# Moving the second norm's row scaling and the shift of the eight largest scores from VectorE to GpSimd, with the orders of four engines rewritten

## The reference, cut to what matters

```
h = layernorm(x) * (1 + ca) + sa
x = x + ga * attention(rmsnorm(h) * norm_w)     # 16 heads of 64, causal, gated by sigmoid(x @ Wg)
h = layernorm(x) * (1 + cb) + sb                # (x - m) / sqrt(v + 1e-5): the second norm
x = x + gb * (mlp(h) + experts(h))
```

## Time and profile before

| | us |
|---|---|
| median of 3 runs (lowest, highest) | 1511.75 (1511.45, 1513.72) |
| the profiled execution's own time | 1514.42 |
| its span from first to last instruction | 1512.6 |
| busy: PE, PE weight loads | 1405.7, 1151.4 |
| busy: DVE, ACT, POOL | 1356.1, 1242.2, 1082.9 |
| mean granted TensorE clock, share of full | 0.976 |

### The profile page before, as it was taken

One profiled execution on the slowest core, in us unless ns is written; L12 is line 12 of the kernel. 1 busy time (PEld: TensorE's weight loads), 2 busy tenths in 40 slices (PEclk: granted clock), 3 DMA queues, 4 the chain that ended last, 5 costly groups with the idle time before them and its releaser, 6 DMA issues.

```text
span 1512.6 us, 39371 instructions
## 1 busy us (share of the span) xinstructions
PE 1405.7 (93%) x11361; PEld 1151.4 (76%) x11361; DVE 1356.1 (90%) x5366; ACT 1242.2 (82%) x4103; POOL 1082.9 (72%) x1201
## 2 busy tenths in 40 slices
PE   3789999999999999999999999999999999999963
PEld 2567888887788887778888777887887788788742
DVE  5579999999999999999999999999999999999853
ACT  1788888988888898888889888888988888888831
POOL 2017877777787777778777777877777787777786
PEclk7999999999999999999999999999999999999976
DMA  5000000000000000000000000000000000000000
GB/s 129 15 13 6 20 20 19 16 19 14 9 19 19 19 16 19 14 9 19 19 19 16 19 14 9 19 19 19 16 19 14 9 19 19 19 16 12 13 8 7
DMA packets 50880, 27.86 MB, mean 18 GB/s; under 512 B 10304, under 2 KB 50048, under 8 KB 50848
## 3 DMA queue, kind: packets, MB, share of 16 engines
q1 hardware_dynamic: 50608, 27.05, 6.9%
q10 hardware_dynamic: 240, 0.43, 0.1%
HBM read 23.15 MB, written 4.31 MB: 18 GB/s over the span
## 4 chain that ended last, share of the span: by engine, by line
PE 60%; DVE 25%; issue 5%; ACT 5%; POOL 3%; DMA 1%; DVEq 0%; POOLq 0%; ACTq 0%
PE pS L1054 9%; PE pW L996 9%; PE pW L998 7%; PE pW L997 7%; PE pW L1067 6%; PE pS L1044 5%; DVE pS L764 5%; DVE h L862 5%; PE pS L1040 4%; ACT pS L534 4%; PE pW L1128 4%; PE pW L1131 4%; PE pW L1071 2%; DVE p_sb L784 2%; PE pW L1119 2%
## 5 line engine op out<-in xcount | busy, mean ns | idle before, releaser
L534 ACT ACTIVATE pS<-pS,nmx 128x128 f32<-128x128 f32 (+1 forms) x1024 | 390.4, 441 | 53.7 <-DVE nmx L764 53.7
L427 POOL TENSOR_TENSOR fexp<-fexp,fsum 128x512 f32<-128x512 f32 x256 | 320.6, 1283 | 80.6 <-DVE fexp L900 80.6
L764 DVE CUSTOM_DVE_ANT_0 pS<-pS,mask 128x128 f32<-128x128 f32 (+1 forms) x1024 | 330.1, 390 | 23.3 <-PE pS L1044 22.8
L418 POOL TENSOR_TENSOR fsum<-ex 128x512 f32<-128x512 f32 x256 | 257.6, 1043 | 0.0
L526 ACT COPY pT<-pS 128x768 f32<-128x768 f32 x256 | 211.7, 827 | 36.0 <-PE pS L1054 31.5
L1054 PE MATMUL pS<-ident,p_sb 128*128 128x128 f32 x1536 | 216.3, 277 | 10.4 <-DVE p_sb L784 6.5
L784 DVE TENSOR_TENSOR p_sb<-pS,coef 128x256 f32<-128x256 f32 (+2 forms) x512 | 210.5, 453 | 8.9
L1054 PEld LDWEIGHTS pS<-ident,p_sb 128*128 128x128 f32 x1536 | 173.3, 141 | 41.5 <-issue 13.5
L534 ACT ACTIVATION_READ_ACCUMULATOR pS<-pS,nmx 128x1 f32 x1024 | 202.2, 197 | 0.0
L434 POOL TENSOR_TENSOR fexp<-fexp 128x512 f32<-128x512 f32 x128 | 172.1, 1364 | 0.2
L516 ACT COPY qk<-pW 128x512 f32<-128x512 f32 x256 | 166.7, 651 | 6.0 <-PE pW L998 6.0
(11 more groups left out here) (164 smaller groups left out, 3642.0 us busy)
## 6 DMA issues: line engine op xcount, KB each, us to landing
x_in<-in_L_attn_tokens SPq DMA_DIRECT2D x32, 128.0 KB, 2.1
modA<-mods_dram SPq DMA_DIRECT2D x32, 128.0 KB, 3.1
x_res<-in_L_attn_tokens SPq DMA_DIRECT2D x32, 128.0 KB, 3.0
modB<-mods_dram SPq DMA_DIRECT2D x32, 128.0 KB, 2.9
out<-yo SPq DMA_DIRECT2D x32, 128.0 KB, 1.9
modC<-mods_dram SPq DMA_DIRECT2D x32, 64.0 KB, 3.0
fsum<-in_L_attn_Wkv SPq DMA_DIRECT2D x2, 512.0 KB, 6.5
fsum<-in_L_attn_Wq SPq DMA_DIRECT2D x1, 512.0 KB, 4.7
```

Source lines behind the costliest of these rows:

```text
L418: ins = nc.gpsimd.tensor_tensor(fsum[:, k, h], ex[:, k, h, 0:NX].unsqueeze(2).broadcast_to([P, NX, NK]), ex[:, k, RH + h, :].unsqueeze(1). ...
L427: ins = nc.gpsimd.tensor_tensor(fexp[:, k, h, :], fexp[:, k, h, :], fsum[:, k, h].rearrange("p i j -> p (i j)"), ALU.mult)
L534: ins = nc.scalar.activation(ps, ps, ACT.Exp, bias=nmx[:, p % 2, h, k:k + 1], scale=-1.0, accum_out=den(p)[:, h, k:k + 1])
L764: ins = nc.vector.tensor_tensor_reduce(out=ps, in0=ps, in1=mask[:, (1 - k) * P:2 * P], scale=-1.0, scalar=LARGEST, op0=ALU.add, op1=ALU.mi ...
```

## The change

`ln2_modulate` disappears from DVE. POOL's `rstd2` becomes `normalise2`, which also does the two row-block instructions. DVE's `shift` no longer makes `top_d`; POOL's new `shift_tops` does, started by a semaphore that the MAX8 instructions set. The orders of DVE, ACT and PE and the bank table are rewritten; POOL's order only gains `shift_tops` after `rms1`. The helper semaphores change to match (`rstd2_out` goes, `pool_chain2` counts 2, `top_s_ready` is new, `HEAD_LINKS` 4 becomes 2).

```diff
@@ GpSimd
+                def shift_tops():
+                    if w.live(-1):
+                        pool.wait_ge(S(top_s_ready), at(top_s_ready, f, TB))
+                        t = top_s[:, :, :, :].rearrange("p a h n -> p (a h) n")
+                        nc.gpsimd.tensor_tensor(top_d[:, :, :, :].rearrange("p a h n -> p (a h) n"), t, t[:, :, 0:1].broadcast_to([P, 2 * TB * RH, TK]),
+                                                ALU.subtract).then_inc(S(top_d_ready), 1)
...
-                        nc.gpsimd.tensor_tensor(rs2[:, :], ve2[:, :], expo[:, :], ALU.pow).then_inc(S(rstd2_out), 1)
+                        nc.gpsimd.tensor_tensor(rs2[:, :], ve2[:, :], expo[:, :], ALU.pow).then_inc(S(pool_chain2), 1)
+                        pool.wait_ge(S(pool_chain2), at(pool_chain2, f, 2))
+                        apart()
+                        for k in range(TB):
+                            ins = nc.gpsimd.tensor_scalar(h2[:, k, :], x2[:, k, :], mv2[:, k, 0:1], rs2[:, k:k + 1], ALU.subtract, ALU.mult)
+                        ins.then_inc(S(h2_ready), 1)
...
-                rstd2()
+                normalise2()
                 weigh(1)
                 rstd1()
                 add_heads(1)
                 rms1()
+                shift_tops()
                 fold(1)
@@ VectorE
-                def ln2_modulate():
-                    if w.live(-1):
-                        dve.wait_ge(S(rstd2_out), at(rstd2_out, f, 1))
-                        for k in range(TB):
-                            ins = nc.vector.tensor_scalar(h2[:, k, :], x2[:, k, :], mv2[:, k, 0:1], rs2[:, k:k + 1], ALU.subtract, ALU.mult)
-                        ins.then_inc(S(h2_ready), 1)
...
-                        link(ins, head_chain, f)
+                        ins.then_inc(S(top_s_ready), 1)
+                        dve.wait_ge(S(top_s_ready), at(top_s_ready, f, k + 1))
...
-                        if k == TB - 1:
-                            nc.vector.tensor_tensor(top_d[:, :, :, :], top_s[:, :, :, :], top_s[:, :, :, 0:1].broadcast_to([P, 2, TB * RH, TK]),
-                                                    ALU.subtract).then_inc(S(top_d_ready), 1)
-                            done(head_chain)
```

More of the change, by code:

```diff
@@ L190, in program @@
         rstd1_in, rstd1_out = ev("rstd1_in", 2), ev("rstd1_out", 2)
-        pool_chain1, pool_chain2 = ev("pool_chain1", 2), ev("pool_chain2", 1)
+        pool_chain1, pool_chain2 = ev("pool_chain1", 2), ev("pool_chain2", 2)
         xr_ready = ev("xr_ready", 1)
@@ L198, in program @@
         x2g_ready = ev("x2g_ready", 1)
-        rstd2_in, rstd2_out = ev("rstd2_in", 1), ev("rstd2_out", 1)
+        rstd2_in = ev("rstd2_in", 1)
         h2_ready = ev("h2_ready", 1)
-        top_d_ready, tops_ready = ev("top_d_ready", 1), ev("tops_ready", 1)
+        top_s_ready, top_d_ready, tops_ready = ev("top_s_ready", TB), ev("top_d_ready", 1), ev("tops_ready", 1)
         cand_ready, rz_ready = ev("cand_ready", 1), ev("rz_ready", 1)
@@ L211, in program @@
         y_gated = ev("y_gated", 1)
-        order = [("V", 0, 0), ("QK", 2, 0), ("QK", 3, 0), ("V", 3, 0), ("PV", 6, -1), ("GU", 1, -2),
[5 rows of a table removed]
+        order = [("V", 0, 0), ("PV", 6, -1), ("QK", 2, 0), ("V", 3, 0), ("QK", 3, 0), ("GU", 1, -2),
[5 rows of a table added]
         assert len(order) % NW == 0, len(order)
@@ L463, in rms1, with normalise2 @@
                         nc.gpsimd.tensor_tensor(rr1[:, :], me1[:, :], expo[:, :], ALU.pow).then_inc(S(rstd1_out), 1)
-                def rstd2():
+                def normalise2():
                     if w.live(-1):
@@ L619, in body @@
                 copy_transposes(7, -1)
+                values(0)
+                weighted(6)
                 queries(2)
-                values(0)
+                values(3)
+                exp_scores(0)
                 queries(3)
-                exp_scores(0)
-                weighted(6)
-                values(3)
                 gate_up(1)
@@ L628, in body @@
                 weighted(7)
+                values(1)
+                scale_head(1)
                 down_tanh(0)
-                scale_head(1)
                 copy_transposes(0, 0)
+                copy_transposes(1, 0)
                 down_tanh(1)
-                copy_transposes(1, 0)
+                values(4)
                 gate_up(2)
-                values(1)
                 exp_scores(2)
@@ L639, in body @@
                 exp_scores(3)
-                copy_transposes(2, 0)
                 weighted(1)
+                gate_up(3)
                 queries(4)
                 scale_head(3)
-                gate_up(3)
+                copy_transposes(2, 0)
                 queries(5)
+                values(2)
                 copy_transposes(3, 0)
-                values(4)
                 modulate_h()
@@ L650, in body @@
                 exp_scores(4)
+                exp_scores(5)
+                weighted(2)
+                weighted(3)
+                scale_head(5)
                 queries(6)
-                weighted(2)
-                values(2)
-                exp_scores(5)
+                values(5)
                 queries(7)
-                values(5)
-                scale_head(5)
-                weighted(3)
                 copy_transposes(4, 0)
@@ L661, in body @@
                 total(1)
+                experts(0)
                 weighted(4)
@@ L664, in body @@
                 rms_scale()
-                experts(0)
                 expert_exp(1)
@@ L668, in body @@
                 weighted(5)
+                exp_scores(6)
                 experts(1)
-                exp_scores(6)
                 exp_scores(7)
@@ L856, in ln2_stats @@
                         ins.then_inc(S(rstd2_in), 1)
-                def ln2_modulate():
-                    if w.live(-1):
-                        dve.wait_ge(S(rstd2_out), at(rstd2_out, f, 1))
-                        for k in range(TB):
-                            ins = nc.vector.tensor_scalar(h2[:, k, :], x2[:, k, :], mv2[:, k, 0:1], rs2[:, k:k + 1], ALU.subtract, ALU.mult)
-                        ins.then_inc(S(h2_ready), 1)
+                        done(head_chain)
                 def shift(k):
@@ L926, in body @@
                 normalise(1)
+                choose(1, 0)
                 gated_down(0)
-                choose(1, 0)
+                choose(1, 1)
+                row_max(2)
+                bias_product(2)
+                row_max(3)
                 gated_down(1)
-                row_max(2)
-                row_max(3)
-                bias_product(2)
+                gate_product(2)
+                ln2_stats()
                 normalise(2)
-                ln2_stats()
-                gate_product(2)
-                choose(1, 1)
                 normalise(3)
                 ln1_stats()
-                ln2_modulate()
                 bias_product(3)
@@ L945, in body @@
                 normalise(4)
+                normalise(5)
                 shift(0)
-                normalise(5)
                 ln1_modulate()
@@ L954, in body @@
                 finish()
+                normalise(7)
                 bias_product(0)
-                normalise(7)
                 gate_product(0)
@@ L1138, in body @@
                 transpose_scores(7, -1)
+                weigh_values(6)
                 project_qk(2)
-                project_qk(3)
                 project_v(3)
                 scores(1)
-                weigh_values(6)
+                project_qk(3)
                 gate_up(1)
+                project_v(1)
                 weigh_values(7)
                 project_down(0)
-                project_v(1)
                 transpose_scores(0, 0)
+                project_v(4)
                 project_down(1)
@@ L1156, in body @@
                 weigh_values(1)
-                transpose_scores(2, 0)
                 project_qk(4)
@@ L1160, in body @@
                 project_qk(5)
-                project_v(4)
+                project_v(2)
+                transpose_scores(2, 0)
+                transpose_h()
                 transpose_scores(3, 0)
                 scores(4)
-                transpose_h()
                 scores(5)
                 weigh_values(2)
+                weigh_values(3)
                 project_qk(6)
-                project_v(2)
                 similarity(0)
@@ L1171, in body @@
                 project_qk(7)
-                weigh_values(3)
                 transpose_scores(4, 0)
-                similarity(1)
                 transpose_scores(5, 0)
                 transpose_experts(0)
+                similarity(1)
                 weigh_values(4)
@@ L1181, in body @@
                 transpose_x()
+                project_ffn(0)
                 transpose_experts(1)
-                project_ffn(0)
                 project_ffn(1)
@@ L1194, in _ @@
             run(pe, body)
-LN1_LINKS, ATTN_LINKS, HEAD_LINKS, TAIL_LINKS, SU_LINKS = 4, NP, 4, 2, 8
```

(1 more changed line is left out.)

## The result

The changed kernel took 1518.07 us (median of 5 runs, 1517.76 to 1519.3) against 1511.93 for the kernel before in the same session: ratio 1.0036, 95% interval 1.0025 to 1.0048. It is slower by 0.4%, beyond the 0.2% that can be told. I had forecast 1503 and a gain. The time lies inside the wide range that I gave (1486 to 1521), but on its slower side.

A forecast was written before the change was run, and what follows sets the result against it. No engine was free: PE allowed about 1.0 us a step, lost on a DVE stretch held up by POOL. A step of 44.15 less 0.25 to 0.3, over 32 steps, gave 8.6 us: 1511.75 to 1503, range 1486 to 1521.

The forecast's parts named there:

- signs of being wrong: h2's instructions near 0.74 us or more, L828 to L833 long, masks still 0.54, or PE idle before similarity(0) or scores.
- The walk: One step followed from scores 1 to scores 6: ln2_stats 1.4 us later, h2 1.7 earlier, scores 6 at 723.3 against 723.61.
- I take 0.40, near the low end: POOL's price in us for each of two 128x128 h2 instructions; 0.80 for both, range 0.68 to 1.48.
- a lead of 0.3: PE reaches scores 6 0.3 us sooner; carried over, a step is 0.25 to 0.3 us shorter.
- The estimate by the Trainium skill: GpSimd at about twice VectorE's time: 1.36 us for the h2 pair, losing up to 0.4 us a step.
- Removed from DVE, 3.6 us: h2's two instructions (2.32 us) and top_d (1.27) leave DVE's 41.9 us a step, leaving about 38.3.
- The masks: choose(1,1) before rm2 meets POOL's large instructions: four masks take 4.4 us instead of 3.1, ln2_stats 1.4 us later.
- Rival (a): Masks held up less than walked, only ACT and PE bound: 0.6 to 0.9 us a step gained, 1483 to 1493; chance 0.22.
- Rival (c): Masks held up in full, POOL's later additions may meet ln1_modulate: slower, likely 1518 to 1528, at most 1540; chance 0.21.
- top_d: On POOL 0.45 us, delaying fold(1) by 0.5; covered by ET1 behind the first half of the feed-forward matmuls (1.8 us).
- ACT's copy before V5: PE waits 0.35 us for V5's bank before scores 6, since PV2's copy now stands behind exponentials 5.
- Filling and draining: Outside the steady steps: same pieces at uncovered prices, DVE's 0.32 against POOL's 0.40; under 1 us, taken as nothing.

The follow-up runs named there:

- after_h_half: Changed kernel with each h2 instruction on GpSimd doing 64 of the 128 columns, the other half of h2 a constant; 1503.96 us, ratio 0.9942.
- after_mask_late: Changed kernel with choose(1,1), the second pair of masks, moved from in front of row_max(2) to behind normalise(3); 1505.74 us, ratio 0.9956.
- after_pv2_early: Changed kernel with ACT's copy of PV2 in front of the exponentials of pair 5 instead of behind them; 1518.00 us, ratio 1.0031.
- after_h_on_dve: Changed kernel with h2 done by DVE again, behind ln1_stats, and rstd2 on POOL; 1611.53 us, ratio 1.0641.
- both_old_order: Kernel before with both moves (h2 and top_d to GpSimd), its old orders and bank table kept; 1516.52 us, ratio 1.0030.

## Why the prediction was wrong

The sign was wrong: faster was forecast, by 0.25 to 0.3 us a step, and it is 0.3 slower. Of the signs of being wrong that I had named, the first came: h2's instructions at 0.74 or more. The walk can be checked point by point. Scores 1 start at 692.32 in the kernel before and 691.80 after, so the changed kernel's times are moved by 0.52 us:

| event | before | forecast | measured, moved |
|---|---|---|---|
| row maximum 2 starts | 701.46 | 703.2 | 703.07 |
| ln2_stats starts | 705.81 | 707.2 | 706.84 |
| PE starts on h | 712.77 | 711.0 | 711.64 |
| exponentials 4 start | 714.89 | 714.6 | 715.15 |
| scores 6 start | 723.61 | 723.3 | 723.91 |

**The step that failed** is one term of the sum, "I take 0.40, near the low end, since only one operand is a tensor; 0.80 for both". It is 0.804 each, 1.60 for both. Up to ln2_stats the walk is right within 0.4 us and on the late side; at h it is 0.6 too early, and this error stands nearly unchanged at exponentials 4 and scores 6 and turns a lead of 0.3 into a lag of 0.3. From ln2_stats to h I had walked 3.8 us and it is 4.8: 0.8 of that is the pair, the rest small excesses in the statistics, the roots and the waits between them. after_h_half changes the pair alone: 0.43 us less in it brings the step 0.46 down, below the kernel before. Each instruction is beyond my upper row too (739 for two tensor operands of twice the size): the reason given, one tensor operand, was no reason. The estimate by the Trainium skill, GPSIMD Engine Reference, section "Performance versus the Vector engine", 1.36 for the pair, was nearer than mine, and the runs exceed it too. I had written that by it the lead would lose up to 0.4 a step; that sentence alone would have led to no gain. My range for the term did end at 1.48, where by the same walk the lead is gone too (0.68 us more than I took, against a lead of 0.28).

**Removed from DVE, 3.6 us: right.** L862 and L878 are gone, and the rest of their cost was the wait for POOL's instructions: undone in the new orders, either is long again.

**The masks: right in size, too weakly drawn.** 4.4 us for four was walked, 4.43 measured, and ln2_stats came 1.0 later against 1.4 forecast. But the experiment says that this one move costs 12 us, nearly as much as after_h_half takes away. Rival (a) put a kernel with less waiting there 0.6 to 0.9 us a step below the kernel before, which is 0.3 to 0.6 below my walk; after_mask_late is 0.38 below the changed kernel. Rival (c), longer waits for the masks, did not occur; its other part, ln1_modulate meeting POOL's later additions, left a trace (the pair took 0.73 instead of 0.60) and no more; its two-input additions (now L843, L844) ran while POOL was waiting and kept their 0.42. So the result lies where rival (c) had its likelier half (1518 to 1528) by luck: the slower side came by none of my mechanisms, but by a term that lay even beyond the bound of 1.48 that I had written down.

**top_d: right for the new orders** (0.40 against 0.45, covered behind the first half of the feed-forward), and the cover that I named is what counts: in the old order, without it, the same instruction costs 14 us. That `top_d` back on DVE would cost 26 in the new orders, through ACT's copy of ET1, I had not seen.

**ACT's copy before V5:** I counted a PE wait there (0.35, measured 0.83) as part of the path. after_pv2_early shows that it isn't.

**Filling and draining,** taken as nothing, gained up to 7.5 us. The draining share is the new orders': behind the last `x2g` come 28.8 to 29.1 us in all five kernels with the old orders, with or without the moves, and 25.3 to 26.6 in all nine with the new ones. The time to the first `x2g` scatters too much to say (121.8 to 124.8 us with the old orders, 119.7 to 124.1 with the new). By the 11.2 us that the steps lost alone the change would have been 0.7% slower.

What a move is worth is set by the order around it. In the old orders h2's move gains 7.6 us and top_d's loses 13.8; in the new orders undoing top_d's costs 26 us more and undoing h2's 93. The new orders without either move were not run.

## What to carry to other kernels

Where several instructions stand on one chain, price the one new form by the top of its bound, not by the plausible middle, if the sign hangs on it. Here even the top of mine was too low, so a form that no row has should be measured alone first. Three forms on VectorE (the masks, h2 and `top_d`) that met a GpSimd instruction here cost what was left of that one, so such a one should be put where GpSimd is idle or in small work: moving one pair of masks so was worth 12 us. It isn't all of VectorE: the batch statistics (L829 and L864) ran beside GpSimd's h2 and its product of `fold(0)` in the steady steps, and none of the 128 took more than 296 ns. When work moves to another engine's queue, look at what stands behind it there: one exchange of two calls was worth about 10.5 us.

## What was not expected of the hardware

GpSimd's `tensor_scalar` with two scalars read from SBUF takes 804 ns for 128 columns and 587 for 64: 3.4 ns a column and 370 ns besides. Its two-tensor instructions take 402 ns for 128 columns (`top_d`), 739 for 256 and 1283 for 512 (`weigh`), 2.1 ns a column above 256. The form with one tensor operand was the dearer one, twice `top_d` for the same 128 columns, while a cast of 512 columns took 609. The kernel before had a hint that I overlooked: L443, a `tensor_scalar` of one column with a scalar read from SBUF, took 302 ns (median), and L461, two columns with constants, a mean of 191. That is a dearer start, but not the dearer column. Whether the scalars from SBUF or the two operations make it so was not tried.

In after_h_on_dve an idle time of TensorE of 2.6 us was followed by a granted clock of 0.5 for about 3.5 us in most steps (twice as long in a few), but not in four, whose idle time was as long. What sets those four apart is not shown. both_old_order, which idles for 1.1 us before ET1 in every steady step, kept 1.00 from 600 to 952 us.
